# Graph layers on one core: the left-over path moved by seven half-chunks, row parts made beside the turning, table clears and loads moved ahead of a barrier

## The reference

```python
h = relu(layernorm(x))
# attention layer
z = (h @ W)
score = z[src] @ a_src + z[dst] @ a_dst
e = exp(-leaky_relu(score, 0.2)) * edge_weight
x = x + elu(segment_sum(e[:, None] * z[dst], src) / segment_sum(e, src))
h = relu(layernorm(x))
# three message layers
for i in range(3):
    msg = relu(h[src] + edge_attr)
    aggr = segment_sum(msg, dst)
    t = relu(bn((h + aggr) @ W1[i] + b1[i]))
    t = bn(t @ W2[i] + b2[i])
    h = relu(t) if i != 2 else t
out = x + h
```

## Time and profile before

| | |
|---|---|
| time, median of 3 runs | 4825.21 us (4821.34 to 4827.64) |
| profiled execution, its own time | 4826.38 us |
| its span in the profile | 4824.7 us |
| sort stage ends (SP's barrier) | 793.8 us from the span's start |
| attention | 803 to 2019 us |
| layer 0, 1, 2 | about 2020 to 2980, to 3902, to 4824.7 us |

### The profile page before, as it was taken

The page is one execution under the profiler, slowest core; times in us unless marked ns, Lnnn a source line. Parts: engine busy times, 40 slices in busy tenths (PEclk is TensorE's granted clock), DMA queues, the critical chain, the costliest instruction groups (busy, mean ns, idle before and its releaser), DMA issues.

```text
span 4824.7 us, 143705 instructions
## 1 busy us (share of the span) xinstructions
PE 4257.5 (88%) x50439; PEld 4143.0 (86%) x50440; DVE 4048.8 (84%) x7870; ACT 2655.3 (55%) x6749; POOL 3255.8 (67%) x2584
## 2 busy tenths in 40 slices
PE   2576676699999999789999997999999979999998
PEld 2566675699999999779999996999999969999996
DVE  7899996477777777678888887888888888888887
ACT  3899996377777777633344345334333454434434
POOL 0488883577777777557777773677777537777763
PEclk7777777799999999889999999999999989999999
DMA  9957663999899888678888884888888848888884
GB/s 123 263 187 242 205 217 124 306 251 251 248 249 250 252 249 248 176 239 278 281 280 279 280 280 149 265 280 281 278 277 281 265 151 279 281 279 280 280 281 148
DMA packets 664741, 1183.55 MB, mean 245 GB/s; under 512 B 151850, under 2 KB 489596, under 8 KB 664588
## 3 DMA queue, kind: packets, MB, share of 16 engines
q1 hardware_dynamic: 450204, 839.07, 53.1%
q10 hardware_dynamic: 133200, 176.14, 15.0%
q0 software_dynamic: 81184, 166.43, 11.0%
HBM read 967.32 MB, written 214.44 MB: 245 GB/s over the span
## 4 chain that ended last, share of the span: by engine, by line
PE 69%; DVE 16%; issue 6%; SPq 5%; DVEq 2%; ACT 1%; DMA 1%; POOL 0%; ACTq 0%; POOLq 0%; PEld 0%; PEldq 0%
PE ps L1766 23%; PE ps L1752 16%; PE ps L1681 12%; PE ps L1668 10%; PE ps L1776 6%; DVE sums L1159 2%; DVE field L1159 2%; DVE dst_hot L1452 2%; DVE sums L1460 2%; DVEq L1465 1%; SPq L552 1%; PE ps L1818 1%; DVE blk_hot L1151 1%; DVE scan L1196 1%; DVE rank L1213 1%
## 5 line engine op out<-in xcount | busy, mean ns | idle before, releaser
L774 POOL DMA_INDIRECT unit_x<-gin_rows,unit_src x1449 | 1785.1, 1232 | 701.8 <-PE ps L1766 456.8
L729 POOL DMA_INDIRECT attr_by_slot<-abuf,ridx x1080 | 1411.7, 1307 | 534.9 <-issue 327.4
L1766 PE MATMUL ps<-dst_hot,sums 128*128 128x128 f32 x10584 | 1519.8, 284 | 84.7 <-DVE agg L1467 84.7
L969 ACT ACTIVATE sums<-sums 128x512 f32<-128x512 f32 x1512 | 834.0, 572 | 1283.0 <-DVE sums L1460 1279.2
L1766 PEld LDWEIGHTS ps<-dst_hot,sums 128*128 128x128 f32 x10584 | 1306.4, 192 | 103.0 <-DVE agg L1467 86.1
L1752 PE MATMUL ps<-x_parts,src_turned 128*128 128x128 bf16 x15876 | 1143.0, 220 | 37.4 <-POOL x_parts L761 33.2
L1752 PEld LDWEIGHTS ps<-x_parts,src_turned 128*128 128x128 bf16 x15876 | 1026.8, 99 | 56.9 <-issue 41.6
L1460 DVE TENSOR_TENSOR sums<-ps,sums 128x512 f32<-128x512 f32 x1512 | 903.7, 615 | 131.2 <-PE ps L1752 127.5
L1452 DVE TENSOR_TENSOR dst_hot<-iota_one,dl_slot 128x896 f32<-128x896 f32 x756 | 818.2, 1082 | 2.2 <-DVE agg L1505 2.2
L881 ACT ACTIVATE val<-ps,val 128x128 f32<-128x128 f32 x2597 | 717.9, 375 | 185.2 <-DVE val L1305 185.2
L1681 PE MATMUL ps<-val,src_hot 128*128 128x129 f32 x5194 | 694.7, 283 | 2.2 <-DVE sums L1245 1.0
(11 more groups left out here) (243 smaller groups left out, 4361.3 us busy)
## 6 DMA issues: line engine op xcount, KB each, us to landing
sums<-attr_by_slot SPq DMA_DIRECT2D x756, 448.0 KB
src_turned<-rows_by_group SPq DMA_DIRECT2D x756, 224.0 KB
turned_hot<-rows_by_block ACTq DMA_DIRECT2D x392, 384.0 KB
attr_by_slot<-zeros SPq DMA_DIRECT2D x36, 3136.0 KB
unit_attr<-in_edge_attr SPq DMA_DIRECT2D x204, 448.0 KB
abuf<-in_edge_attr SPq DMA_DIRECT2D x72, 960.0 KB
unit_x<-gin_rows,unit_src POOLq DMA_INDIRECT x1449
attr_by_slot<-abuf,ridx POOLq DMA_INDIRECT x1080
```

The costliest lines, as they stand in the source:

```text
L729: pool.indirect_dma_start(out=attr_table, out_offset=bass.IndirectOffsetOnAxis(ap=ridx[:, g, t0 + t:t0 + t + 1], axis=0), in_=abuf[:, k % ...
L774: pool.indirect_dma_start(out=unit_x[:, half_place(k), t, :], out_offset=None, in_=gin_rows[n], in_offset=bass.IndirectOffsetOnAxis(ap=uni ...
L969: act.activation(attr[:, first:first + tiles, :], attr[:, first:first + tiles, :], ACT.Relu).then_inc(s_msg, 1)
L1766: ins = pe.matmul(ps[:, 7, 0:WINDOW], attr[:, b, :], dst_hot[:, HOT[c], b % G_TILES, :], start=(b == 0), stop=(b == BLOCKS - 1))
```

## The change

Four edits.

1. The left-over path of a message layer stays in group 1 but stands ahead of half 8 (`LEFT_HALF`) in place of half 0, on DVE, ACT and PE. SP issues its loads between the two loads of chunk 6 of group 1, in place of behind chunk 2.
2. For layers 1 and 2, chunks 0 and 1 of the row parts are made beside the turning: ACT's parts stand behind its chunks 5, 7, 8 and 12 of the second normalisation, DVE's two `rest` behind its copies 6 and 10. The first part of chunk 2 stands behind ACT's last chunk. Layer 0 keeps its order.
3. The 34 clears are spread over the first 14 loads (`CLEAR_LOADS`) and not over 19.
4. `SORT_LOADS` is 18 (from 16) and `LOADS_THEN` 20 (from 19): loads 16 and 17 stand ahead of the barrier, two loads and no clear stand between the windows and the attention's left-over loads. The bases of 12 windows (`HELD`) are read ahead of the barrier.

```diff
-LOADS_THEN = 19
-SORT_LOADS = 16
+LOADS_THEN = 20
+SORT_LOADS = 18
+CLEAR_LOADS = 14
+HELD = 12
-LEFT_GROUP, LEFT_CHUNK = 1, 2
+LEFT_GROUP, LEFT_HALF = 1, 8
+FIRST_PARTS, REST_PARTS, SECOND_PARTS = (5, 8), (6, 10), (7, 12)
...
                 if k == SORT_LOADS:
+                    held = {g: window_base(g) for g in range(EARLY * A_TILES, EARLY * A_TILES + HELD)}
                     sp.wait_ge(s_fld, GROUPS)
...
-                for g in range(k * (BUCKETS - FILLS_FIRST) // LOADS_THEN, (k + 1) * (BUCKETS - FILLS_FIRST) // LOADS_THEN):
-                    clear_slots(g + FILLS_FIRST)
+                for g in range(k * (BUCKETS - FILLS_FIRST) // CLEAR_LOADS, (k + 1) * (BUCKETS - FILLS_FIRST) // CLEAR_LOADS):
+                    if g + FILLS_FIRST < BUCKETS:
+                        clear_slots(g + FILLS_FIRST)
...
                 def group_of(i, parts=False):
-                    if isinstance(i, int) and i == LEFT_GROUP:
-                        left_message()
                     for h in range(G_HALVES):
+                        if isinstance(i, int) and i == LEFT_GROUP and h == LEFT_HALF:
+                            left_message()
...
                         normalise(m, c)
+                        if m == 1 and n + 1 < LAYERS:
+                            if c in FIRST_PARTS:
+                                first_part(n + 1, FIRST_PARTS.index(c))
+                            if c in SECOND_PARTS:
+                                second_part(n + 1, SECOND_PARTS.index(c))
...
+                if n + 1 < LAYERS:
+                    first_part(n + 1, PART_LEAD)
...
                     ins.then_inc(s_copied, 1)
+                    if n + 1 < LAYERS and c in REST_PARTS:
+                        rest(n + 1, REST_PARTS.index(c))
```

More of the change, by code:

```diff
@@ L632, in load_chunk @@
                              sources[at, c * G_TILES * P:(c + 1) * G_TILES * P].rearrange("o e -> (o e)").partition_broadcast(P)).then_inc(s_lo[c], 16)
+                if isinstance(g, int) and g == LEFT_GROUP and c == G_CHUNKS - 1:
+                    load_left(((gidx[:, 0, :], left_src), (gidx[:, 1, :], left_dst), (gidx[:, 2, :], left_eid), (gsm[:, 0, :], left_v)),
+                              s_lg[n]["loaded"], s_lg[n]["done"])
                 sp.wait_ge(s_used, G_HALVES * done + 2 * c + 2 - G_HALVES + G_HALVES)
@@ L938, in _ @@
             act.wait_ge(s_small, 128)
-            for n in range(LAYERS):
[L941 to L964, removed]
@@ new lines, in _, with first_part @@
+            rows = flat[:, :].rearrange("p (b d) -> p b d", d=D)
+            def first_part(n, c):
+                of = slice(c * G_TILES, (c + 1) * G_TILES)
+                last = min((c + 1) * G_TILES - 1, BLOCKS - 1) // BY_CHUNK
+                if n == 0:
+                    for t in (last - 1, last):
+                        normed(act, t)
+                else:
+                    act.wait_ge(s_copied, TURNS[f"gin_out{n - 1}"] + last + 1)
+                act.activation(x_parts[:, 0, of, :], rows[:, of, :], ACT.Copy).then_inc(s_part, 1)
@@ new lines, in second_part @@
+            def second_part(n, c):
+                of = slice(c * G_TILES, (c + 1) * G_TILES)
+                act.wait_ge(s_rest, G_CHUNKS * n + c + 1)
+                act.activation(x_parts[:, 1, of, :], unit_x[:, c % 2, :, :], ACT.Copy).then_inc(s_part, 1)
+            first_part(0, 0)
+            for c in range(PART_LEAD):
+                for t in range(c * CHUNKS // PART_LEAD, (c + 1) * CHUNKS // PART_LEAD):
+                    keep_columns(t)
+                second_part(0, c)
+                first_part(0, c + 1)
@@ L1519, in group_of @@
                             if first and c + PART_LEAD < G_CHUNKS:
-                                rest(c + PART_LEAD)
+                                rest(n, c + PART_LEAD)
                             if c + TURN_LEAD < G_HALVES // 2:
@@ L1533, in group_of @@
                             add_unit(i, k)
-                rest(0)
+                if n == 0:
+                    rest(0, 0)
                 for c in range(TURN_LEAD):
                     turn_sources(0, c)
-                rest(1)
+                if n == 0:
+                    rest(0, 1)
                 group_of(0, True, first=True)
@@ L1784, in group_of @@
                 def group_of(i, more):
[L1785 to L1786 removed]
                     for h in range(G_HALVES):
+                        if isinstance(i, int) and i == LEFT_GROUP and h == LEFT_HALF:
+                            sum_left_messages()
                         if h + G_LEAD < G_HALVES:
```

35 lines of the change are left out of this document (16 added, 19 removed).

## The result

The changed kernel takes 4780.89 us (median of 4 runs, 4776.45 to 4785.12); the kernel before took 4825.72 us beside it, 44.8 us more. The ratio is 0.991 with a 95% interval of 0.9898 to 0.9922. The forecast was 4771 us, its range 4752 to 4790. The profiled execution took 4777.09 us with a span of 4775.4, against 4826.38 and 4824.7: 49.3 us less, where the sum said 54.3.

What follows compares the result with a forecast made beforehand. The prediction took places where PE stands as the bound: attention's left-over path, group 1's start and layer starts. 4826.38 - 40.5 - 14.7 + 0.9 = 4772.1, less 1.2 to the median: 4771 us, range 4752 to 4790.

Steps and rivals of the forecast that it cites:

- Attention, -40.5: Attention's left-over path: PE's 36.12 us hole shrinks to the path's own steps, sums at 907.4 against 947.88, -40.5 us.
- The windows' term: Windows behind the barrier: 12 bases read early save 0.50 us each, 6.0 us, all passed on to PE.
- The path's own 7 us: Attention's left-over path: from PE's matmul 2.1 us to DVE's next chunk and 5.0 more to PE's sums.
- nothing pays for them in the sort: Sort: six more clears ahead of the barrier add at most 8.8 us a load's step, DMA share below 1; taken as 0.
- Left-over path of the layers, -14.7: Group 1 of three layers: 29.7 us of stall removed, 15.0 us new at half 8, net -14.7 us.
- No DMA is waited for: Layers' path at half 8: gathered rows land about 8 us into group 1, DVE needs them at about 10.
- about 4 us, sum 5.0: Layers' path at half 8: chain of about 4 us, PE fills 0.8; with reader idle and lost lead 5.0 a layer.
- The bound of 8.5: Layers' path at half 8: upper bound per layer, from the old stall behind the landing and a lower clock.
- costs at half 8 what it did at half 0: Rival on the layers' left-over path: PE's lead is lost in mid-group, 4771 + 14.7 = 4786 us; chance 0.12.
- Row parts, +0.9: Starts of layers 1 and 2: row parts beside the turning cost net 0.45 us each, +0.9 us.
- The slower rival: Sort: clears slow POOL's scatters from 2.53 to 3.0 us each, 4771 + 102 = 4873 us; chance 0.02.

Runs made afterwards that it cites:

- stand_in_clears: Kernel before with all clears behind the first 14 loads, plus iotas for POOL's scatters from load 16 on and the units' gathers: 4789.32 us.
- stand_in_mended: Changed kernel, layers' left-over loads behind chunk 2, row parts reordered, iotas for POOL's scatters from load 18 on and units' gathers: 4793.43 us.
- queue_only: Changed kernel with the layers' left-over path and row parts put back, leaving the edits on SP's queue around the barrier: 5307.61 us, ratio 1.0004 to kernel before.
- clears_only: Kernel before with one edit, all clears of the attribute table behind the first 14 loads: 5218.85 us, ratio 0.9977 to kernel before.
- before_again: Kernel before, unaltered, run again with a profile on a third chip: 5223.93 us, ratio 0.9988 to kernel before.
- after_again: Changed kernel, unaltered, run again beside the kernel before on another chip: 5262.99 us, ratio 1.0058.
- stand_in_after: Changed kernel with iotas in place of POOL's scatters from load 18 on and of the units' gathers: 4803.09 us.

## Why the prediction was right, and where not

**Attention, -40.5.** Right, for the reason given; measured 42.9 at the path and 44.0 at the attention's end. The clears, the loads and the windows went as the working had them (windows done at 829.96 for 829; POOL's gathers at 879.4 for 875, since load 18 came 8.9 us behind its issue and not 5; small loads out at 850 for "before 870"). The windows' term is larger than 6.0: PE ended block 2 8.1 us earlier, though its first sums came 2.5 us later (816.3 for 813.8). The path's own 7 us stayed. That the clears do most of it is shown by stand_in_clears, within its two reserves; that nothing pays for them in the sort holds nearly on the chip of the first profiles, where the windows began 0.7 us later and PE's first sums the 2.5 us above.

**Left-over path of the layers, -14.7.** This is the term that failed: it measured -5.9. The part that was taken away was sized rightly (30.7 us in the three layers for 29.7, of which 9.6 in layer 1 for 9.9): from group 0's last sums to group 1's addition it would be 24.0 us without a stall, the 1.66 us to group 0's addition (2963.49 to 2965.15) and a group without its unit, 23.82 - 1.5. The part that comes anew is 24.8 us by the same measure and not 15.0. Two steps of it are wrong. "No DMA is waited for" rested on loads issued ahead of group 0's end; SP issues them behind `src_turned` of chunk 6, whose wait is for PE's last gathers of group 0, and with POOL's issue and 7.9 us to the landing the rows come 13.4 us into group 1, not 8. And "about 4 us, sum 5.0" left out that PE's first matmuls behind a stall run at the lower clock: at half 8 the step to group 1 is 30.75 us (30.25 in layer 2) against 23.82 - 1.5 without a stall, so 8.4 us, and with the rows long there (stand_in_mended) still 7.0. The bound of 8.5, made from the landing and the lower clock, was the right figure. The rival "costs at half 8 what it did at half 0" came nearer: 9.6 against 8.4 in layer 1. It had a chance of 0.12.

**Row parts, +0.9.** Mis-sized: about +1.0 at each of two layer starts, +2. I saw ACT's wait behind chunk 7 and not the one behind chunk 12 (2.01 us): second part 1 waits for the rest that DVE does behind copy 10, and the copies come at ACT's pace. stand_in_mended shows that the order was at fault, not the idea: with it a layer start is 1.9 to 2.5 us quicker.

**The sum.** 54.3 were forecast for the profiled execution and 49.3 came: 8.5 less from the layers (5.3 against 13.8), 3.5 more from the attention. The layers' 5.3 us are 5.9 of the path, 1.8 at layer 0's start, -2.0 of the row parts and -0.5 spread over the stretches behind. That the two errors have opposite signs is luck, and it is part of why the time came out so near. Between the medians it is 44.8 us: the forecast put the median 1.2 us under the profiled execution, and it came 3.8 us above it. The runs of the changed kernel lie at 4776.5 and 4777.1, and at 4784.7 and 4785.1; only one of the lower ones has a profile, so what parts them stays open.

**The slower rival** (scatters of the sort hurt by the clears) did not occur on the first chip. What occurred on the others was not among the rivals: scatters and gathers of POOL that hold up the other engines.

Open: why some chips have this and one had not, and by what way POOL's indirect DMAs hold the others up. The DMA packets' own times don't differ (scatters' packets 97 ns in the median in the first profile after, 96 in after_again). The rows name only "issue" and "remote" for these waits. No single edit was measured on a chip like the first, so there the layers' terms are read from the two profiles alone. And each chip was used at one time only, so that it is the chip that matters, and nothing else that differed, is not shown.

## What to carry to other kernels

Ask of a transfer that is queued ahead of a critical one whether it must be there; taking the clears out of the way was one edit and 34.8 of the 49.3 us. Measure a moved stall between marks that lie outside both its old and its new place, and price its restart at the lower clock. A chain that is set beside another engine's pace should be walked to its last member: the second wait is as long as the first. And measure on more than one chip: the change that won 0.9% on the first lost 0.6% on another, and queue_only, with all the edits that won the attention's 44 us, was level on a third. That shorter bursts of indirect DMAs would help is not shown: clears_only issues 45 scatters behind the barrier, nearly without a break, and was no slower than the kernel before.

## What the runs showed of the hardware

- On 4 chips POOL's indirect DMAs held up PE, DVE and ACT: PE's matmuls in 200 us fell from 2745 (first profile after) to 2146 (before_again), DVE stood 41.3 us (after_again) and ACT 24.0 us (stand_in_after) beside unbroken scatters. With an iota in their place, on the same engine with the same waits, the two kernels took 4803 and 4789 us on a chip where the kernel before took 5290. On the chip of the first profiles scatters at the same pace cost nothing: PE was busy for all of 200 us there.
- Most of PE's waits for "issue" on these chips are not fetches of instructions over the DMA queues. The Trainium skill, page Runtime: NRT & Kernel Launch, section Instruction fetch mechanics, says that the sequencer fetches its next block over a DMA queue of its own and that this is mostly hidden. The first profile after agrees (no such waits of PE from 1000 to 1800 us, and 5 packets of the instruction queues for all engines). In before_again PE had 169 such waits in the same 800 us, 73.7 us together, and the instruction queues moved no more than this:

```profile
q14 instruction: 4, 0.03, 0.0%
q8 instruction: 1, 0.02, 0.0%
```

  So these waits don't speak against the page, and what PE waits for stays open.
- POOL and DVE stretch each other: POOL's last part of chunk 1 took 3.57 us in place of 1.89 (at 2933.11 in the profile after) beside the end of DVE's three `src_turned` and the `dst_hot` behind them, and the three `src_turned` took 2.60 in place of 1.17 beside POOL's part in stand_in_mended. The Trainium skill, page SBUF — State Buffer, section SBUF: two separate sides, has DVE exclude POOL in a faster mode too, not with two inputs alone. The rows agree: `src_turned` passes 896 columns in 0.44 us, the f32 `dst_hot` in 1.08.
